# The order of an expert's five output blocks in a two-layer mixture-of-experts kernel: the short, branched block goes third

## The reference, cut to what matters

```
# layer 0: top 2 of 8, capacity 560 rows per expert
xg = x_pad[dispatch]                                   # [8, 560, 256]
h  = gelu(einsum('ecd,edf->ecf', xg, w1) + b1)         # [8, 560, 1024]
y  = einsum('ecf,efd->ecd', h, w2) + b2                # [8, 560, 256]
out = segment_sum(y * gate, token)                     # added to x
# layer 1: top 2 of 8, no capacity
h  = silu(x @ w1[e]) * (x @ w3[e])
out = einsum('etf,efh,te->th', h, w2, w)               # added to x
```

## Time and profile before

| what | value |
|---|---|
| time before, median of 3 runs | 1068.19 us (1061.28 to 1068.98) |
| the profiled execution's own time | 1073.41 us |
| its span | 1071.3 us, 22763 instructions |
| what lies around the span | 2.1 us |
| PE busy | 935.2 us (87%) |
| DVE / ACT / POOL busy | 686.6 / 546.8 / 463.3 us |
| mean granted clock of PE | 0.929 |
| experts 0 on PE | about 410 to 624 us of the span |
| experts 1 on PE | about 751 to 1064 us of the span |

### The profile page before, as it was taken

How to read it: one execution, slowest core, us unless ns; L and a number is a source line. 1 busy time by engine, 2 the same in 40 slices (tenths; PEclk the granted TensorE clock), 3 DMA queues, 4 the chain that set the end, 5 groups by cost and what they waited for, 6 DMA issues and landing times.

```text
span 1071.3 us, 22763 instructions
## 1 busy us (share of the span) xinstructions
PE 935.2 (87%) x7879; PEld 851.5 (79%) x7879; DVE 686.6 (64%) x1947; ACT 546.8 (51%) x1208; POOL 463.3 (43%) x438
## 2 busy tenths in 40 slices
PE   5889998998899856899899939982999999999997
PEld 4678787787778646899899936662999999999977
DVE  6456665575557566767767627874667877787443
ACT  3668877786788745555555514330333433333220
POOL 2022224232522224767666642545354455455514
PEclk8999999898899877999999979895899999999999
DMA  6878887787756316777977676644453354335101
GB/s 187 169 202 191 202 202 194 213 183 190 163 141 158 79 56 191 193 193 175 224 169 175 149 180 172 199 151 141 166 143 97 100 139 112 93 107 139 21 5 22
DMA packets 110035, 160.21 MB, mean 150 GB/s; under 512 B 11600, under 2 KB 98992, under 8 KB 107984
## 3 DMA queue, kind: packets, MB, share of 16 engines
q1 hardware_dynamic: 95968, 140.16, 49.6%
q0 software_dynamic: 13936, 18.33, 8.9%
HBM read 103.45 MB, written 56.96 MB: 150 GB/s over the span
## 4 chain that ended last, share of the span: by engine, by line
PE 44%; DVE 7%; DMA 5%; issue 4%; POOL 2%; ACT 1%; another core or an unknown queue 0%; SPq 0%; POOLq 0%; DVEq 0%
PE ps L323 37%; DMA x_scratch<-XG 2%; DMA XG<-xg_scratch 2%; DVE HTH L1346 2%; PE ps L514 2%; PE ps L602 1%; PE ps L619 1%; POOL x_scratch L1614 1%; PE ps L670 1%; DVE WL L953 1%; DMA X<-x_scratch 1%; PE ps L337 1%; PE ps L342 0%; POOL xg_scratch L1550 0%; DVE r_sel L964 0%
## 5 line engine op out<-in xcount | busy, mean ns | idle before, releaser
L323 PE MATMUL ps<-XGH,WH 128*128 128x280 f32 (+1 forms) x768 | 219.7, 286 | 2.6 <-DVE GT L1342 2.2
L323 PE MATMUL ps<-XGL,WH 128*128 128x280 f32 (+1 forms) x768 | 221.2, 288 | 0.0
L323 PE MATMUL ps<-XGH,WL 128*128 128x280 f32 (+1 forms) x768 | 220.8, 288 | 0.0
L1218 DVE CUSTOM_DVE_ANT_0 NS<-ps,negm 112x375 f32<-112x375 f32 x256 | 138.0, 546 | 110.9 <-PE ps L429 103.4
L1602 POOL TENSOR_TENSOR HTL<-GT,HTH 128x280 fp32r<-128x280 f32 x112 | 116.3, 1039 | 161.4 <-DVE HTH L1346 161.4
L775 ACT ACTIVATE PP<-NS,MN 112x375 f32<-112x375 f32 x256 | 156.4, 611 | 4.0 <-DVE MN L1218 3.5
L437 PE MATMUL ps<-cst,PP 112*125 112x112 f32 x768 | 141.0, 295 | 19.4 <-ACT PP L775 14.5
L323 PE MATMUL ps<-WH,HTH 128*128 128x256 f32 (+1 forms) x536 | 152.9, 285 | 2.5 <-DVE XG L1359 2.5
L323 PE MATMUL ps<-WL,HTH 128*128 128x256 f32 (+1 forms) x536 | 150.9, 281 | 0.0
L323 PEld LDWEIGHTS ps<-XGH,WH 128*128 128x128 f32 x768 | 147.5, 192 | 3.6 <-DVE GT L1342 2.8
L323 PE MATMUL ps<-WH,HTL 128*128 128x256 f32 (+1 forms) x536 | 150.3, 280 | 0.0
(11 more groups left out here) (211 smaller groups left out, 1891.8 us busy)
## 6 DMA issues: line engine op xcount, KB each, us to landing
WG<-in_v SPq DMA_DIRECT2D x48, 512.0 KB
KST<-k_scratch SPq DMA_DIRECT2D x48, 376.0 KB, 5.5
WG<-in_w SPq DMA_DIRECT2D x32, 512.0 KB
k_scratch<-KHL SPq DMA_DIRECT2D x64, 188.0 KB
CT<-in_ctx_t SPq DMA_DIRECT2D x32, 375.0 KB, 6.0
xg_scratch<-zero SPq DMA_DIRECT2D x8, 1289.8 KB
xg_scratch<-zero SPq DMA_DIRECT2D x16, 586.2 KB, 9.5
XG<-xg_scratch SPq DMA_DIRECT2D x14, 536.0 KB, 3.8
```

The lines of the kernel that those rows point to most:

```text
L323: m = e.matmul(out_ap, l, r, start=n == 0, stop=n == len(steps) - 1)
L1218: e.tensor_tensor_reduce(out=NS[:, n % 4, :], in0=ps[0:S, n % 3, 0:KEYS], in1=negm[:], scale=1.0, scalar=3.0e38, op0=ALU.add, op1=ALU.min, ...
```

## The change

A table gives the order of an expert's blocks: 0, 1, 4, 2, 3. The short block, with the branch around its products, now stands at place 2; blocks 2 and 3 are at places 3 and 4. All engines follow the table. Everything that belonged to a place and not to a block keeps its place: the turn of the PSUM banks, the pieces of transposes (before places 0, 2 and 4), the waits for the hidden halves (places 0 and 2), the weight work, the semaphores of the scatters. What is computed is the same.

```diff
+ROW_ORDER = (0, 1, 4, 2, 3)
...
         def row_block(layer, n):
 
-            ex, c = divmod(n, 5)
-            return ebufs[layer][0][0:rows_of(c), ex % 2, c, 0:D]
+            c = ROW_ORDER[n % 5]
+            return ebufs[layer][0][0:rows_of(c), n // 5 % 2, c, 0:D]
...
-            def rows_out(ex, c, full):
-                n = 5 * ex + c
+            def rows_out(ex, i, full):
+                n, c = 5 * ex + i, ROW_ORDER[i]
                 bk = 4 + n % 2
                 if n >= 2:
                     e.wait_ge(y_out[layer], n - 1)
...
-                if c in (0, 2):
-                    n_dve, n_pool = hl_of((ex * 2 + c // 2) * 8 + 7)
+                if i in (0, 2):
+                    n_dve, n_pool = hl_of((ex * 2 + i // 2) * 8 + 7)
...
-                for c in range(4):
-                    if ex + 1 < E and c in (0, 2):
-                        transposes(ex + 1, c)
-                    rows_out(ex, c, True)
-                if ex + 1 < E:
-                    transposes(ex + 1, 4)
-                with e.If(e.value_load(fl[0:1, layer, ex:ex + 1], min_val=0, max_val=1)):
-                    rows_out(ex, 4, True)
-                with e.Else():
-                    rows_out(ex, 4, False)
+                for i in range(5):
+                    if ex + 1 < E and i in (0, 2, 4):
+                        transposes(ex + 1, i)
+                    if ROW_ORDER[i] < 4:
+                        rows_out(ex, i, True)
+                    else:
+                        with e.If(e.value_load(fl[0:1, layer, ex:ex + 1], min_val=0, max_val=1)):
+                            rows_out(ex, i, True)
+                        with e.Else():
+                            rows_out(ex, i, False)
...
-            def rows_gated(ex, c):
-                n = 5 * ex + c
+            def rows_gated(ex, i):
+                n, c = 5 * ex + i, ROW_ORDER[i]
...
-            def rows_done(ex, c):
-                n = 5 * ex + c
+            def rows_done(ex, i):
+                n, c = 5 * ex + i, ROW_ORDER[i]
...
-            def rows_added(ex, c):
-                n = 5 * ex + c
+            def rows_added(ex, i):
+                n, c = 5 * ex + i, ROW_ORDER[i]
```

More of the change, by code:

```diff
@@ L543, in rows_out @@
                     e.wait_ge(y_out[layer], n - 1)
-                if layer == 1 and ex == E - 1 and c == 0:
+                if layer == 1 and ex == E - 1 and i == 0:
                     e.wait_ge(o_y, 1)
-                if c == 0:
+                if i == 0:
                     for k in range(2):
                         e.wait_ge(*wl_of(base + per * ex + per - 2 + k))
-                if c in (0, 2):
-                    n_dve, n_pool = hl_of((ex * 2 + c // 2) * 8 + 7)
+                if i in (0, 2):
+                    n_dve, n_pool = hl_of((ex * 2 + i // 2) * 8 + 7)
                     e.wait_ge(hl_dve[layer], n_dve)
```

## The result

| | kernel before | changed kernel |
|---|---|---|
| median of 10 runs each | 1068.59 us (1061.28 to 1070.16) | 1077.02 us (1070.59 to 1081.83) |
| the profiled execution | 1073.41 us, span 1071.3 us | 1070.71 us, span 1068.5 us |
| mean granted clock of PE | 0.929 | 0.933 |

The ratio is 1.0065, with a 95% interval of 1.0041 to 1.0089: slower by 4.4 to 9.5 us (the medians differ by 8.4), less than the 1% that counts as a difference here. The forecast was 4.9 us slower, 1073.1.

A forecast was written before the change was run, and what follows sets the result against it. PE was taken to bound both expert stages, with holes in layer 0 mainly from waits for gathered rows. Layer 0's +6.2 and layer 1's -1.3 made +4.9 us on 1068.19, so 1073.1 us; range 1064 to 1082.

The forecast's parts named there:

- The sum: Whole kernel: 6.2 us lost by the end of layer 0 and 1.3 gained in layer 1, +4.9 us.
- The bank wait: PE before block 2 waits until DVE has emptied block 1's shared PSUM bank: 9.2 us in layer 0, 1.85 in layer 1.
- the correction for DVE's being 0.8 earlier: Layer 0, where PE doesn't wait: block 1 taken out 7.4 us after the hidden products end, not 8.2; 0.8 an estimate.
- the walk: Layer 0: following PE's loop and the scatter-and-gather loop expert by expert to see how much stall shows, 6.2 us.
- The clock loss: Expert 0 of layer 0: two pauses parted by a single matmul lower PE's clock, 1.5 us, bounds 0 and 3.
- What the holes take in: Layer 0: of 9.2 + 1.5 us new cost, 6.2 show at its end; the rest falls into existing holes.
- I keep its clock loss: Layer 0, expert 3: the hole shrinks from 3.65 to 2.2 us, but the lower clock behind it was assumed to stay.
- The scatter: Each expert's last adding scatter carries 128 rows, not 48: 0.9 us more where the gather ends last, bounds 0.17 and 1.85.
- Rival B: Scatter-and-gather loop takes the change in full: gathers 1.85 us later each, 11.1 us, +14 in all, 1082; chance 0.14.
- Rival A: Layer 0's holes hide the waits and the ends gain: expert 0 costs 1.3, -0.8 to -4.7 us in all; chance 0.2.
- Rival C: DVE is in time for block 1, stalls stay near 0.3 us, layer 0 unchanged: 1067.6 us; chance 0.14.
- Layer 1: Three waits on DVE go (-2.2), bank stalls add 1.85, the kernel's end gains 0.95: -1.3 us.

The follow-up runs named there:

- the third group: Runs beside a kernel before at 1045.64 us; the changed kernel, unedited, came out there at ratio 1.0043.
- its repetition: The changed kernel run once more with nothing edited, against the kernel before: ratio 1.0070.
- own_bank: Changed kernel, but the short block goes to PSUM bank 3, so block 2 no longer waits for block 1: ratio 0.9983 to the kernel before.
- expert0_filled: Changed kernel, but at expert 0 of layer 0 the short block's 24 matmuls run although the flag is not set: ratio 1.0016 to the kernel before.
- layer1_own_bank: Kernel before with the new order in layer 1 only, the short block there in PSUM bank 3: ratio 0.9973 to the kernel before.
- old0_weights_later: As layer1_own_bank (old order in layer 0), but layer 0's weight steps stand behind places 2 and 3: ratio 1.0074 to the kernel before.
- before_again: The kernel before run once more with nothing edited, for a second profile: 1038.01 us in its one run.

## Why the prediction was right

The sum was +4.9 us. The stages say +5.8 in layer 0, -0.1 in layer 1 (312.5 in the mean of four against 312.6), -1.3 in the tail: +4.4, and the time +4.4 to +9.5. In the third group, where the ratio is 1.0043, that is 4.5 us of 1045.64 and the stages carry it all. In the first comparison and its repetition the medians differ by 8.4 and 7.1 us and the ratios say 6.9 and 7.5, 2.5 to 4 us more than the stages. No trace shows where: layer 0 starts anywhere from 407.6 to 415.4 us in that group, whatever the expert order is. This remains open. That the sum lies within 0.5 us of the stages is in part luck: it kept 1.4 us of an old clock loss that went, and it made the bank wait 0.9 us too small.

**The bank wait: confirmed.** Forecast 2.9, 0.5, 2.05, 1.65 and 1.25 us at experts 0, 1, 2, 3, 5; listed are 2.76, 1.12, 1.18, 0.96 and 1.41. The listing leaves out what hides behind the modelled ends of matmuls. Counted as the forecast was, from the start of the transposes ahead of place 2 to block 2's first matmul, less the 0.52 us that this takes without a wait, it is 1.6, 1.5, 1.5, 0.4 and 1.6 at experts 1 to 5, 0.5 at expert 7 and 2.9 at expert 0: 10.1 us where 9.2 were forecast. After the correction for DVE's being 0.8 earlier it was to be 1.3, 1.3, 1.9 and 0.5 at experts 1, 2, 3 and 5. The lag from the next expert's first transposes to block 1's taking out came out at 7.7 us at all four (460.71 - 452.96 = 7.75 at expert 1), where I had put 7.4. That estimate nearly held, but the walk then doubted the evenness: it gave expert 3 1.9 and expert 5 0.5 from the late and the early blocks of the old trace (its gather at 538.3 also follows only from a lag of 8.0). With an even lag the stall is even. Own_bank, which takes this wait away in both layers, takes the loss in time with it; its layer 0 keeps 2.3 us of the 5.8.

**The clock loss: confirmed, with its size.** Forecast 1.5 us; expert0_filled measures 1.3. The Trainium skill (TensorE: Matmul & The Clock Gate, "HAM oscillation — how this bites in real kernels") says that such waits throttle the array. The traces agree for two pauses with a lone matmul between them. The 2.46 us pause alone left the clock at 1.00.

**What the holes take in: confirmed, but for experts 3 and 4.** By the walk, the first transposes of the next expert were to come 2.8, 4.1, 4.2, 4.4, 5.3 and 5.8 us later, and layer 0's end 6.2. Counted from each trace's first hidden product plus the 5.61 us between these, they came 2.8, 4.6, 4.6, 4.3, 2.5 and 4.2 later, and the end 4.9 (5.8 in the means). One step that failed is "I keep its clock loss" at expert 3: its hole shrank from 3.65 to 1.64 us and the half clock behind it went. From the transposes behind this hole to those ahead of place 2 it was 7.54 us before (533.90 to 541.44) and is 6.14 after (532.59 to 538.73), a gain of 1.4 us. So one clock loss came and another went, and only the one that came is in the sum. The other is that expert 4's gather would be waited for with 0.9 us added; there the hole was gone.

**The scatter: right at some experts, not as one number.** I added 0.9 us for a last scatter of 128 rows instead of 48. From POOL's start to SP's gather the mean is 3.65 us in the four traces with the old order and 3.95 in the four with the new, only 0.3 more. But the mean hides opposite signs. At experts 0 to 5 the old order has 3.0, 2.6, 3.6, 6.1, 4.0 and 2.6 us, the new one 4.1, 3.2, 3.7, 6.1, 2.8 and 3.7: 0.6 to 1.2 more at experts 0, 1 and 5, nothing at expert 3, as I had said, and 1.2 less at expert 4. The last goes with the hole that was gone there; what shortens it is open. In the tail the last scatter starts 3.04 us after PE's end before and 1.31 after, and the span ends 4.07 and 4.48 us behind that start. So it gained 1.73 us by the earlier start and lost 0.4, where I had put 1.85 and 0.9: 1.3 and not 0.95. Rival B, with its full 1.85 at each gather, needed over 5 us at most experts and holes above 4; only expert 3 is above 5, as it was before, and the longest hole is 1.64. Rival A had the holes right and expert 0 wrong: 4.2 us are lost there, where it gave 1.3. Rival C falls with the listed waits.

**Layer 1: confirmed.** The three waits of 2.2 us went, and the small stalls cost 2.2 (312.5 against the 310.3 of own_bank, layer1_own_bank and old0_weights_later) where 1.85 were counted, with one of 0.46 at expert 7. The Trainium skill (SBUF — State Buffer, "SBUF: two separate sides") calls the clash of the earlier trace rows an exclusive lock. The new trace agrees in two ways. With POOL's step earlier the cast is at its usual length, 0.40 us, and not somewhat long, as a mere slower rate would have left it. And DVE's weight step took 4.27 us instead of 1.22 where it met POOL's 2.97 us step, and ended 1.09 us after it. In both clashes DVE's instruction is the blocked one although its recorded start is the earlier (by 0.53 and 0.21 us); recorded starts on POOL are rough, so who came first is not shown.

## What to carry to other kernels

A short or skipped block placed between two long ones takes away the cover of whatever the second long one shares with the first, here a PSUM bank; look for the resource one or two places back, and give the short block its own before moving it. A stall that lies ahead of a hole in the same loop mostly falls into the hole, so cost it by walking both loops, and look hardest at the place with no hole behind it and a pause already in front. Moving the step that makes a buffer late only helps if the place that it moves to has room: here POOL's step, behind place 3, held up the last scatter and cost as much. A mean over experts can hide effects of opposite sign; look at each before calling a term small.

## What the runs showed of the hardware

- **The clock depends on more than the length of a pause.** Behind a single pause of 2.4 to 2.5 us at expert 0 the granted clock stayed at 1.00 in seven traces. In own_bank it fell to 0.50 behind a hole of 2.22 us and stayed at 1.00 behind one of 3.26; in before_again it stayed up behind 2.93, in layer1_own_bank it fell behind 2.71. Behind 2.46 + 2.76 us with one matmul in between it was 0.50 and 0.78. A lone matmul did not keep it up; 24 did.
- **What a last scatter of 128 rows costs over one of 48 depends on where it falls.** To SP's next gather it was 0.6 to 1.2 us more at three experts, 0 to 0.1 at two and 1.2 less at one; 0.4 at the end of the kernel. 0.17 us is POOL's own share.
- **POOL's weight step held up some of DVE's instructions and not others.** Beside POOL's 2.99 us step at 900.25, DVE's instruction that takes rows out of PSUM took its usual 0.48 us; the cast of the earlier trace rows took 3.67 instead of 0.33 to 0.40, and DVE's weight step 4.27 instead of 1.22.
- **The same program runs 24 us shorter in other groups of runs**, almost all of it in the attention ahead of layer 0, and the changed kernel's ratios in the groups, 1.0065, 1.0070 and 1.0043, agree within their intervals.
